# The decay arguments of a state-space layer, made by ScalarE instead of TensorE

## The reference, cut to what matters

```python
dt = softplus(dt + dt_bias);  A_dt = -exp(A_log) * dt
A_cumsum = cumsum(A_dt, axis=-1)                 # within a chunk, per head
Lmat = exp(segment_sum(A_dt))                    # exp(cum[l] - cum[s]) for s <= l, else 0
Y_diag = (C B^T * Lmat) @ (x * dt)
decay_states = exp(A_cumsum[..., -1:] - A_cumsum)
states = B^T (decay_states * x * dt)
new_states[c] = exp(A_cumsum[c, -1]) * new_states[c-1] + states[c-1]
Y_off = (C @ new_states) * exp(A_cumsum)
y = rmsnorm(Y_diag + Y_off + D * x) * silu(gate) @ out_proj
```

## Time and profile before

| | |
|---|---|
| median of 3 runs | 2142.29 us (2140.72 to 2142.93) |
| the profiled execution | 2141.5 us |
| its span, first to last instruction | 2139.8 us |
| TensorE busy | 2102.7 us, 98% |
| VectorE busy | 1689.4 us, 79% |
| ScalarE busy | 1401.8 us, 66% |
| GpSimd busy | 881.4 us, 41% |
| the mixer's loop, steps 0 to 127 | 322 to 1880 us |

### The profile page before, as it was taken

One profiled execution on the slowest core, in us unless ns is written; L12 is line 12 of the kernel. 1 busy time (PEld: TensorE's weight loads), 2 busy tenths in 40 slices (PEclk: granted clock), 3 DMA queues, 4 the chain that ended last, 5 costly groups with the idle time before them and its releaser, 6 DMA issues.

```text
span 2139.8 us, 37480 instructions
## 1 busy us (share of the span) xinstructions
PE 2102.7 (98%) x13386; PEld 1732.0 (81%) x13386; DVE 1689.4 (79%) x2679; ACT 1401.8 (66%) x1918; POOL 881.4 (41%) x622
## 2 busy tenths in 40 slices
PE   7999998999999999999999999999999999999999
PEld 6788876888888888888888888888888888878887
DVE  7555468988888888888898889898888888876554
ACT  5322277878787777777787877787777778752221
POOL 1222134545454545444454544544544545422221
PEclk9999998999999999999999999999999999999999
DMA  5543224233333333232333333342333233255441
GB/s 201 177 146 138 61 94 125 90 109 103 100 112 101 105 96 108 95 122 91 100 112 101 101 98 114 105 122 96 100 101 112 90 104 109 97 186 177 135 147 40
DMA packets 128644, 241.89 MB, mean 113 GB/s; under 512 B 14048, under 2 KB 48608, under 8 KB 128224
## 3 DMA queue, kind: packets, MB, share of 16 engines
q1 hardware_dynamic: 128480, 239.73, 34.9%
HBM read 234.17 MB, written 5.51 MB: 112 GB/s over the span
## 4 chain that ended last, share of the span: by engine, by line
PE 90%; DVE 3%; issue 3%; ACT 2%; DMA 1%; POOL 1%; SPq 0%; DVEq 0%; POOLq 0%; ACTq 0%
PE ring L1013 35%; PE ring L1113 16%; PE bank L412 6%; PE bank_e L412 6%; PE yt L1094 6%; PE st L1078 4%; PE yt L1100 4%; PE xt L1065 3%; PE bank_e L424 3%; PE bank L424 3%; PE arg L1051 2%; PE xt L1026 1%; PE bank L654 1%; DMA w_raw<-w_in 0%; DVE xr L304 0%
## 5 line engine op out<-in xcount | busy, mean ns | idle before, releaser
L1013 PE MATMUL ring<-m_lnt,w_sb 128*128 128x512 f32 x3456 | 859.9, 399 | 1.2 <-DVE xc L1440 1.2
L1013 PEld LDWEIGHTS ring<-m_lnt,w_sb 128*128 128x128 f32 x3456 | 633.0, 189 | 127.1 <-DVE xc L1440 1.5
L1673 POOL TENSOR_TENSOR w_sb<-w_raw,w_sb 128x512 fp32r<-128x512 f32 x288 | 401.7, 1400 | 177.3 <-ACT w_sb L1246 177.0
L1688 POOL TENSOR_TENSOR ysq<-ysq,y 128x512 f32<-128x512 f32 x126 | 162.8, 1292 | 652.8 <-ACT y L1290 652.8
L1113 PE MATMUL ring<-wo,ygs 128*128 128x512 f32 x1536 | 369.4, 390 | 2.0 <-issue 2.0
L1113 PEld LDWEIGHTS ring<-wo,ygs 128*128 128x128 f32 x1536 | 287.3, 188 | 63.2 <-issue 2.6
L1440 DVE SCALAR_TENSOR_TENSOR xc<-ring,cw,xc 128x511 f32<-128x511 f32 (+2 forms) x384 | 286.0, 745 | 23.0 <-ACT xc L1258 13.9
L1258 ACT ACTIVATE xc<-ring,cb,cw 128x512 f32<-128x512 f32 x128 | 99.2, 775 | 215.4 <-PE ring L1013 215.4
L1678 POOL TENSOR_TENSOR wo<-wo_raw,wo 128x512 fp32r<-128x512 f32 x128 | 214.0, 1672 | 0.0
L1246 ACT ACTIVATE w_sb<-w_raw 128x512 fp32r<-128x512 f32 x288 | 177.0, 619 | 26.8 <-DMA w_raw<-w_in 26.8
L1094 PE MATMUL yt<-em,x_dt 128*64 128x128 f32 x2048 | 183.7, 279 | 3.2 <-DVE state L1482 3.2
(11 more groups left out here) (203 smaller groups left out, 3159.2 us busy)
## 6 DMA issues: line engine op xcount, KB each, us to landing
w_raw<-w_in SPq DMA_DIRECT2D x288, 256.0 KB, 4.2
ce<-e_t SPq DMA_DIRECT2D x128, 384.0 KB, 4.1
wo_raw<-w_out SPq DMA_DIRECT2D x128, 256.0 KB, 4.4
f_gu_q<-gu_w SPq DMA_DIRECT2D x28, 512.0 KB, 3.7
f_gu_zr<-gu_z SPq DMA_DIRECT2D x28, 512.0 KB, 4.5
f_gu_sr<-gu_s SPq DMA_DIRECT2D x28, 512.0 KB, 5.3
f_dn_q<-dn_w SPq DMA_DIRECT2D x28, 256.0 KB, 3.5
f_dn_zr<-dn_z SPq DMA_DIRECT2D x28, 256.0 KB, 4.0
```

What stands on the lines that cost most here:

```text
L1013: mm = nc.tensor.matmul(dst[:], w_sb[:, u % WR, wp, k * P:(k + 1) * P], lnt[:, xp, k, b * S:(b + 1) * S], start=(i == 0), stop=(i == 3 * K ...
L1673: nc.gpsimd.tensor_tensor(w_sb[:, u % WR, 1], w_raw[:, u % NR], w_sb[:, u % WR, 0].bitcast(F32), ALU.subtract).then_inc(w_lo, 1)
```

## The change

- The three bfloat16 parts, their store and their loads, the 8 matmuls of a step and the tiles `a_left`, `a_right` are gone. The cumulative sums are stored once as float32 (`c_t`), and each step loads its two heads' rows broadcast to all 128 partitions into `cum_b` (one buffer, 512 KB written in SBUF).
- ScalarE makes and clamps the arguments: 8 instructions of 128 columns, each `Relu(cum_q - cum_b)` with a column of the token-wise sums `cum_q` as its bias, from SBUF into `ARG`. The Exp and the order of ScalarE's other instructions in a step stay.
- SyncE waits for the clamp of step k (`arg_clamped`) before it loads `cum_b` for step k+1; `ce` (now `load_decay`), `wo_raw` and the next weights come behind that.
- Before the loop, the sums by token, the sums after a token (`later`) and the chunk sums come from six matmuls with triangular and full matrices, and the transposes, differences and products that served for them go, with GpSimd's memsets and products. The order there is changed: `gram(0)` and `turn_b(0)` stand ahead of `project(("x", 2))`, and `dt_q` is copied earlier.

```diff
 def exponent(k):
-    act.wait_ge(arg_mm, k + 1)
+    act.wait_ge(c_loaded, 16 * (k + 1))
+    need(act, em_done, k)
...
+    for h in range(2):
+        for c in range(CPB):
+            at = slice(c * CS, (c + 1) * CS)
+            clamp = nc.scalar.activation(ARG[:, h, at], cum_b[:, h, at], ACT.Relu, scale=-1.0,
+                                         bias=cum_q[:, k, c, h:h + 1])
+    clamp.then_inc(arg_clamped, 1)
     part = ARG[:].rearrange("p h t -> p (h t)")
-    nc.scalar.activation(part, part, ACT.Relu, scale=-1.0).then_inc(arg_clamped, 1)
     act.wait_ge(arg_clamped, k + 1)
     nc.scalar.activation(part, part, ACT.Exp, scale=-1.0).then_inc(exp_done, 1)
...
 def load_args(k):
     b, h = batch(k), 2 * pair(k)
-    sp.wait_ge(a_ones, 4)
-    need(sp, arg_mm, k - 1)
-    for g in range(2):
-        at = 32 * g
-        sp.dma_start(a_right[at:at + 3, k % 2], a_parts[0:3, h + g, b * S:(b + 1) * S])\
-            .then_inc(a_loaded[k % 2], 16)
-        sp.dma_start(a_left[at + 3:at + 6, k % 2], a_parts[0:3, h + g, b * S:(b + 1) * S])\
-            .then_inc(a_loaded[k % 2], 16)
+    need(sp, arg_clamped, k)
+    sp.dma_start(cum_b[:], c_t[h:h + 2, b * S:(b + 1) * S]
+                 .rearrange("(o h) t -> o h t", o=1).to_broadcast([P, 2, S])).then_inc(c_loaded, 16)
+
+def load_decay(k):
+    b, h = batch(k), 2 * pair(k)
...
 for k in range(K):
     if k > 0:
-        load_units(k + 1)
+        load_units(units_of(k + 1))
     if k + 1 < K:
         load_args(k + 1)
+        load_decay(k + 1)
...
 for k in range(STEPS):
...
-    if k < K:
-        arguments(k)
     if 1 <= k <= K:
         outputs(k - 1)
```

Before the loop, on TensorE:

```diff
 project(("z", 0))
 cumulate()
+for b in range(B):
+    cumulate_by_token(b)
+sum_later(0)
 project(("x", 1))
+sum_later(1)
+sum_chunks()
 project(("z", 1))
-project(("x", 2))
 gram(0)
 turn_b(0)
-turn_dec()
-spread_last()
+project(("x", 2))
```

More of the change, by code:

```diff
@@ L8 @@
 F32R = mybir.dt.float32r
-BF16 = mybir.dt.bfloat16
 I32 = mybir.dt.int32
@@ L930, in sync, with load_units @@
             def sync(self, sp, tiles):
-                def load_units(k):
-                    for unit in units_of(k):
+                def load_units(units):
+                    for unit in units:
                         u = UNIT[unit]
@@ L1023, in gram @@
                         pe.wait_ge(xdt_done, k + 1)
+                    else:
+                        pe.wait_ge(decq_done, 1)
                     dst = gram_bank(n)
@@ L1040, in turn_b @@
                     mm.then_inc(btok_mm, 1)
-                def arguments(k):
-                    pe.wait_ge(a_loaded[k % 2], 64 * (k // 2 + 1))
-                    need(pe, em_done, k)
-                    if k == 0:
-                        pe.wait_ge(btok_done, 1)
-                        pe.wait_ge(decq_done, B)
-                    for c in range(CPB):
-                        for g in range(2):
-                            rows = slice(32 * g, 32 * g + 6)
-                            mm = nc.tensor.matmul(ARG[:, g, c * CS:(c + 1) * CS],
-                                                  a_left[rows, k % 2, c * CS:(c + 1) * CS],
-                                                  a_right[rows, k % 2, c * CS:(c + 1) * CS], start=True, stop=True)
-                    mm.then_inc(arg_mm, 1)
                 def turn_x(k):
@@ L1152, in cumulate, with cumulate_by_token, sum_later, sum_chunks @@
                         mm.then_inc(cum_mm, 1)
[L1154 to L1162 removed]
+                def cumulate_by_token(b):
+                    pe.wait_ge(adt_done, b + 1)
+                    pe.wait_ge(dtq_done, b + 1)
+                    nc.tensor.matmul((XT, ST)[b][:], tri[:], a_dt[:, b], start=True, stop=True).then_inc(cumq_mm, 1)
+                def sum_later(b):
+                    pe.wait_ge(later_done, 1)
+                    pe.wait_ge(adt_done, b + 1)
+                    if b:
+                        pe.wait_ge(cum_done, 1)
+                    nc.tensor.matmul((YT, ARG[:, 0])[b][:, 0:OFFC * H], later[:], a_dt[:, b, 0:OFFC * H],
+                                     start=True, stop=True).then_inc(dec_mm, 1)
+                def sum_chunks():
                     pe.wait_ge(cum_done, B)
                     for b in range(B):
[L1165 to L1169 removed]
+                        at = b * (OFFC - 1) * H
+                        mm = nc.tensor.matmul(ARG[:, 1, at:at + (OFFC - 1) * H], ones[:], a_dt[:, b, H:OFFC * H],
+                                              start=True, stop=True)
+                    mm.then_inc(last_mm, 1)
                 project_dt(0)
@@ L1339, in scalar @@
                 nc.scalar.activation(low[:], low[:], ACT.Ln, bias=1.0).then_inc(softplus, 1)
+                for b in range(B):
+                    act.wait_ge(adt_done, b + 1)
+                    nc.scalar.activation(dt_q[:, b * JP:(b + 1) * JP],
+                                         (XT, ST)[b][:].rearrange("p (c j h) -> p j c h", c=CPB, h=2), ACT.Copy)\
+                        .then_inc(dtq_done, 1)
                 w_high(("x", 1))
@@ L1342, in scalar @@
                 tap(("x", 0))
+                for b in range(B):
+                    act.wait_ge(cum_mm, b + 1)
+                    nc.scalar.activation(cum[:, b * S:(b + 1) * S], ARG[:, b], ACT.Copy).then_inc(cum_done, 1)
                 w_high(("z", 1))
@@ L1366, in scalar @@
+                for b in range(B):
+                    act.wait_ge(dec_mm, b + 1)
+                    part = (YT, ARG[:, 0])[b][:, 0:OFFC * H]
+                    nc.scalar.activation(part, part, ACT.Exp).then_inc(dec_exp, 1)
+                act.wait_ge(last_mm, 1)
+                nc.scalar.activation(e_last[:].rearrange("p b c h -> p (b c h)"), ARG[:, 1], ACT.Exp).then_inc(last_done, 1)
+                w_high(("x", 2))
                 tap(("x", 1))
                 copy_btok(0)
-                act.wait_ge(last_mm, 1)
@@ L1536, in vector @@
                     norm_low(dve, nm, t)
+                nc.vector.tensor_scalar(later[:], tri[:], -1.0, 1.0, ALU.mult, ALU.add).then_inc(later_done, 1)
                 conv(("b", 0))
```

143 lines of the change are left out of this document (46 added, 97 removed).

## The result

The changed kernel takes 2231.8 us (median of 4, 2227.94 to 2235.34) against 2141.7 us before (median of 4, 2140.72 to 2142.93): ratio 1.042, 95% interval 1.0401 to 1.0439. It is 90 us slower. The forecast was 2189 us, slower, with a range of 2100 to 2250: the sign and the ring that makes the loss came out; the forecast loss, 47 us, was about half of the measured 90.

What follows compares the result with a forecast made beforehand. TensorE bounds the kernel before; after, a ring of clamps, loads and ScalarE takes 101.5 us a group against 98.69, 43 us over 15.4 groups. With 4 for the first steps, 2141.5 becomes 2188.5, forecast 2189 us, range 2100 to 2250.

Steps and rivals of the forecast that it cites:

- the ring that makes the loss: Clamps release cum_b and the weights queued behind it, which release ScalarE's next w_high and clamps: 101.5 us a group.
- What bounds the kernel before: In the loop TensorE alone sets the pace, busy throughout; a group of eight steps takes 98.69 us.
- TensorE's saving of 0.33 us a step: Removing the argument matmuls saves TensorE 0.33 us a step, 2.6 a group, leaving it 96.0 us a group.
- C, the clamps: ScalarE's time for a step's eight 128-column clamps, which overlap: 2.4 us, bounds 2.15 and 3.2.
- rival 3: The small clamps don't overlap and take 3.2 us, 6.4 us more a group: 2287 us, chance 0.07.
- D, the landing: Time from the clamps' end to the landing of the x weights, with cum_b in front: 7.2 us, ends 6.5 and 8.3.
- rival 1: TensorE stays the bound and the kernel is faster, cum_b landing at the plain price: 2105 us, chance 0.25.
- Ordinary steps: Five steps of a group, each from clamp end to clamp end: D + 2.24 + C = 11.84 us.
- The steps behind the extra weights: Two steps a group, behind the extra weights of B or C, where z's load waits for GpSimd's low part: 14.0 us each.
- The step behind c: One step a group, where ScalarE's late tap of C releases VectorE's convolution, ahead of its Silu: 14.3 us.
- The first steps: Steps 1 to 4, without output tiles: ScalarE's 1.4 us more a step shows in most, +4 us, between 0 and 6.
- Rivals 1 and 2: The second: saving and loss cancel, with D from 6.5 to 6.8; within 0.2%, 2142 us, chance 0.08.

Runs made afterwards that it cites:

- the wait alone: Kernel before, with SyncE's wait ahead of the a_left and a_right loads made a wait for the clamp's end; 2141.9 us, ratio 1.0004.
- the two kernels that reach it: Changed kernel with one 1024-column clamp in place of eight, 2108.4 us; changed kernel with SyncE's loads and ScalarE's order rearranged, 2110.5 us.
- the kernel with ScalarE's order mended too: Changed kernel with SyncE's loads in order of need, Silu of b and c ahead of the clamps, b or c copy behind the exponential; 2110.5 us.
- the Silu moved: Changed kernel with only the Silu of b and c moved from its step's end to just ahead of the next step's clamps; 2214.9 us, ratio 1.0349.
- The quarter load: Changed kernel loading cum_b to only 32 partitions after the first step, 128 KB in place of 512 KB; 2149.0 us, ratio 1.0036.

## Why the prediction was right in kind and short in size

- **What bounds the kernel before.** Right. Reordering loads and ScalarE's work in it changes its groups by 0.1 us; the wait alone by nothing.
- **TensorE's saving of 0.33 us a step.** Right in an ordinary step (11.50 to 11.19, 0.31) and near as a bound: 96.39 and 96.62 us a group in the two kernels that reach it, against 96.0. But a whole group went down to 96.5 in most cases, 2.2 us and not 2.6: the three steps with extra work save less. The idle 0.35 us stayed, now ahead of the weight loads of the outputs:

```profile
1022.18 0.42 PEld L1080 LDWEIGHTS yt<-em,x_dt 128*64 128x64 f32 x8 [0.35 <-issue]
```

  That row is from the kernel with ScalarE's order mended too. By the Trainium skill (TensorEngine Tiling (Array Packing), Key Properties) a change of tiling mode drains TensorE; the trace agrees, with 0.35 us still idle and a saving of 0.31 rather than 0.43.
- **C, the clamps.** Right: 2.40 to 2.41 us for 2.4. They overlap, so rival 3 is out.
- **D, the landing.** Right within its bounds: 6.9 in the step shown, and some 7.35 from the mean of the ordinary steps (11.99 less 2.24 and 2.40), for 7.2. Read in every step, it is 7.3 to 7.5 on the average of each of the five. `cum_b` lands after 4.3 us and `w_raw` after 5.6, as described. Cutting the bytes takes 0.9 us off. The choice of rows for the price of `cum_b` decided this, and the prediction passed over rows of the very size, which the page of the kernel before has:

```profile
f_gu_q<-gu_w SPq DMA_DIRECT2D x28, 512.0 KB, 3.7
f_gu_zr<-gu_z SPq DMA_DIRECT2D x28, 512.0 KB, 4.5
f_gu_sr<-gu_s SPq DMA_DIRECT2D x28, 512.0 KB, 5.3
```

  The last two are broadcasts of one row, issued 0.4 to 0.5 us apart, so they price 512 KB at 1.2 to 1.3 us, which is rival 1's D of 6.5. `cum_b` took some 2.2 (7.35 less 0.04 and 5.14). Its rows are of 2 KB, like those of `f_dn_zr`, and those of `f_gu_zr` of 4 KB; whether that is the reason no run shows. The 2.0 came out well, but nothing in the prediction gave it the preference.
- **The ring and its slopes.** Right: near 8 us a group for each microsecond of clamps (5.7 for 0.75) and 5 for each of landing (5.1 for 0.9).
- **Ordinary steps.** Forecast 11.84; measured 11.9 to 12.2, five of them 0.8 us a group too small, which is D at 7.35 for 7.2.
- **The steps behind the extra weights.** Forecast 14.0 both; measured 14.8 and 14.1. In the first, z's copy stands 6.41 us after that of b (1076.51 to 1082.92) instead of 5.37:

```profile
1076.51 0.62 ACT L1233 ACTIVATE w_sb<-w_raw 128x512 fp32r<-128x512 f32 x1
...
1082.92 0.63 ACT L1233 ACTIVATE w_sb<-w_raw 128x512 fp32r<-128x512 f32 x1 [3.28 <-DMA w_raw<-w_in]
```

  SyncE issues z's load when GpSimd has made the low part of b, here and in the kernel before:

```profile
1079.96 0.33 SPq L932 DMA_DIRECT2D w_raw<-w_in  x1
```

```profile
841.86 0.33 SPq L937 DMA_DIRECT2D w_raw<-w_in  x1
```

  That is 3.45 us after b's copy, where it was 2.75: 0.7 of the 1.04 is GpSimd's, whose low part of b took 2.01 us instead of 1.30. The 3.45 recurs in every group. The rest is z's landing, 2.9 us for 2.6. Why the two took longer stays open.
- **The step behind c: the largest miss.** Forecast 14.3, measured 15.6. I had written that "the slack of TensorE on this chain (a tap 3 us late stops nobody) doesn't help, since it is used up once, not in each group", and so followed the ring through ScalarE and DMA alone. TensorE's timeline in that place, then VectorE's, then ScalarE's:

```profile
1090.67 4.21 PE L1007 MATMUL ring<-m_lnt,w_sb 128*128 128x512 f32 x12 [3.33 <-ACT sz L1255]
...
1105.57 0.83 PE L1060 MATMUL st<-x_dec,b_tok 128*128 128x128 f32 x6
1106.15 3.02 PE L1007 MATMUL ring<-m_lnt,w_sb 128*128 128x512 f32 x12
```

```profile
1106.43 0.29 DVE L1473 COPY state<-st 128x128 f32<-128x128 f32 x1 [2.58 <-PE st L1060]
1106.76 0.98 DVE L1479 SCALAR_TENSOR_TENSOR state<-state,e_last,st 128x64 f32<-128x64 f32 x4
1107.66 2.31 DVE L1438 SCALAR_TENSOR_TENSOR bc<-ring,cw,bc 128x511 f32<-128x511 f32 x3
```

```profile
1105.47 0.77 ACT L1245 ACTIVATE bc<-ring,cb,cw 128x512 f32<-128x512 f32 x1
1110.00 1.06 ACT L1260 ACTIVATE bc<-bc 128x1024 f32<-128x1024 f32 x1 [3.77 <-DVE bc L1438]
```

  In the step ahead of the Silu of b and c (the last row) ScalarE is so late that its Silu of z, which frees a bank of the ring, stops TensorE for 3.33 us. The granted clock is then 0.69 on average from 1090.6 to 1094.9, that is partly at 1.2 GHz, and a projection of 12 matmuls takes 4.21 us instead of 3.02. TensorE stays late, and with it `states` (1105.57). VectorE's queue has the copy of what `states` makes ahead of c's convolution, and VectorE stands 2.58 us for it. So ScalarE taps c in time (1105.47, without idle time), but the convolution begins 2.19 us after the tap, where the forecast had it 0.68 behind, and ScalarE stands 3.77 us for it.

  The other groups separate the stall from the clock. Of the 13 with output tiles in these steps, three kept a clock of 1.00 after stalls of 2.65, 3.13 and 3.33 us. One of them:

```profile
571.54 3.01 PE L1007 MATMUL ring<-m_lnt,w_sb 128*128 128x512 f32 x12 [3.33 <-ACT sz L1255]
```

  There the convolution starts 0.8 us after the tap and the step takes 14.43 us, in each of the three: near the forecast's 14.3. (So does the first group, whose steps have no output tiles yet.) In the other ten, stalls of 3.1 to 4.7 us were followed by 4.3 us at a mean granted clock of 0.50 to 0.68; the convolution starts 2.0 to 3.4 us after the tap and the step takes 15.7 to 17.0. So what the sum lacked goes with the clock that TensorE loses, and not with the stall by itself. In the step shown the projection lost 1.2 us at the lower clock and the first row of the outputs 0.4 (1.04 us for 0.66), about the 1.4 by which the convolution is later than in the three. Why it fell after some stalls of 3.3 us and not after others stays open. The lateness I called harmless is handed round: ScalarE to TensorE to VectorE and back to ScalarE. No run takes the stall away and leaves the rest. With the Silu moved the convolution is as late, but off ScalarE's path, and the step takes 14.2; that this is near the 14.3 of the sum is chance, since other waits fill that step.
- **The first steps.** Forecast +4 (0 to 6), measured +8.4 at the sixth `ce` issue (375.7 against 367.3), out of the bounds. About half of it comes with the wait alone (372.2 in that kernel, +4.9). A like pattern: TensorE stands for VectorE, which had stood for ScalarE's exponential, and runs on at half clock (0.50 from 366.3 to 372.0, the 1.2 GHz level, after 5.5 us of idling).

```profile
366.40 1.12 PE L1076 MATMUL yt<-em,x_dt 128*64 128x128 f32 x8 [5.52 <-DVE state L1479]
```

- **The number of groups.** I multiplied by 15.4; the last 1.4 have no extra weights, and the last full group takes 96.2 us where it took 95.98. It should have been 14 groups, which would have made the forecast 4 us smaller.
- **The sum.** 14 x (104.46 - 98.69) = 81 for the groups (forecast 43), 8.4 for the first steps (4), 0.2 for the last group: 89.4. The last steps and what follows give 3.0 back (forecast: under 1), so that the spans of the two profiled executions differ by 86.4 (2226.2 and 2139.8). The changed kernel's is 3.9 us under its median, which makes it the measured 90. Of the 38 us missing in the groups, 18 are the step behind c (1.3 x 14), 11 the ordinary steps (0.8 x 14), 12 the two others (0.9 x 14), less 4 for the multiplier; they add to 37.

Rivals 1 and 2, with 0.33 of the chance, missed by D: they wanted it under 6.8, and it was 6.9 in the step shown and 7.35 on average. The quarter load, 0.9 us less on D, came within 7 us of the kernel before: it takes little for such a change to turn. With the rows of 512 KB as the price the same sum would have said faster, so the sign owes something to luck.

## What to carry to other kernels

When a load's buffer is freed by the instruction that reads it, everything behind that load on its queue is freed by it too. Write down the ring (reader, queue, landing, next reader) and compare its length with the bound engine's step: below it, the wait is free however large it reads in the profile (179 us here), above it each added microsecond counts in nearly every step. Before moving a load forward, ask of each load behind it in the queue what it will now wait for; and when an engine off the path gets later, look for what it hands out (banks, buffers), since it can stop the bound engine, which may then run on at the lower clock.

## What the runs showed of the hardware that I had not expected

- The cost of a TensorE stall was often more than its length: after 3.33 us of idling twelve matmuls took 4.21 us instead of 3.02 (granted clock 0.69), and after 5.52 us some 5.7 us ran at a granted clock of 0.50. After another stall of 3.33 us the twelve took 3.01, at a clock of 1.00.
- 512 KB broadcast from two rows, ahead in the queue, delayed the loads behind by only 0.9 us more than 128 KB did (5.6 against 4.7 us to landing; 2.8 with neither ahead).
- Splitting a 1024-column ScalarE instruction into eight with a bias each costs 1.3 us (1.11 to 2.40), and four of these into eight of 64 columns another 0.75: 0.18 to 0.19 us for each further instruction.
